# Idle-bank products of ones in eight pauses of TensorE, in a fused four-layer kernel

## The reference

```python
hidden = gelu(x @ down_W.T + down_b)                 # L0: adapter, 256 -> 64
hidden = hidden @ expert_W[idx].T + expert_b[idx] + domain_emb[idx]
x = layernorm(hidden @ up_W.T + up_b + x) * ln_gamma + ln_beta

x = _ln(src) * (1.0 + scale) + shift                 # L1: attention block, 16 heads of 16
scores = q @ k / sqrt(16) + attention_bias           # masked, softmax
x = x + (probs @ v) @ Wo + bo
ff = _gelu2((_ln(x) * g2 + beta2) @ W1 + b1) @ W2 + b2
x = x + ff                                           # L2: then a rotation of groups of four features

probs = softmax(style(norm(x)) @ router_w)           # L3: 8 experts, the best 2 of each token
y = sum over 2 experts of gate * (relu(h @ exp_w1 + exp_b1) @ exp_w2 + exp_b2)
return x + y
```

## Time and profile before

| | us |
|---|---|
| median of 3 runs | 686.25 |
| lowest, highest | 685.91, 686.96 |
| the profiled execution | 689.78 |
| its span | 687.9 |
| TensorE busy (share of the span) | 557.8 (81%) |
| VectorE busy | 468.5 (68%) |
| ScalarE busy | 297.2 (43%) |
| GpSimd busy | 226.5 (33%) |
| mean granted TensorE clock | 0.93 of full speed |

### The profile page before, as it was taken

How to read it: one execution, slowest core, us unless ns; L and a number is a source line. 1 busy time by engine, 2 the same in 40 slices (tenths; PEclk the granted TensorE clock), 3 DMA queues, 4 the chain that set the end, 5 groups by cost and what they waited for, 6 DMA issues and landing times.

```text
span 687.9 us, 15375 instructions
## 1 busy us (share of the span) xinstructions
PE 557.8 (81%) x4840; PEld 413.9 (60%) x4841; DVE 468.5 (68%) x1308; ACT 297.2 (43%) x616; POOL 226.5 (33%) x137
## 2 busy tenths in 40 slices
PE   3719576999597997769949399999789999999992
PEld 1616355558385484654838248676567778777771
DVE  5573796689979979883897935886454646474751
ACT  1615542642564425535243232666364444353540
POOL 0412553207714238133370422122612313122222
PEclk9999668999988999989978599999999999999996
DMA  8583451913066451466606576773532322222220
GB/s 288 127 203 124 156 158 56 226 32 123 1 170 160 131 184 63 130 149 227 200 1 244 210 253 232 274 260 49 171 48 41 50 40 42 33 48 38 43 42 0
DMA packets 41176, 86.49 MB, mean 126 GB/s; under 512 B 7321, under 2 KB 31810, under 8 KB 37026
## 3 DMA queue, kind: packets, MB, share of 16 engines
q1 hardware_dynamic: 21744, 56.77, 24.1%
q0 software_dynamic: 8352, 16.99, 13.4%
q10 hardware_dynamic: 11026, 12.02, 5.9%
HBM read 57.23 MB, written 29.44 MB: 126 GB/s over the span
## 4 chain that ended last, share of the span: by engine, by line
PE 53%; DVE 24%; issue 7%; ACT 5%; DMA 5%; ACTq 3%; POOL 2%; SPq 0%; DVEq 0%; POOLq 0%
PE bank L1918 8%; PE bank L1743 6%; PE bank L1907 5%; PE bank L1909 5%; PE bank L1908 4%; PE bank L1919 4%; PE bank L1642 3%; PE bank L1707 2%; PE bank L1723 2%; DMA stage<-in_moe_w 2%; PE bank L1752 2%; PE bank L1697 2%; ACTq L855 2%; DVE stats L1038 2%; DVE sc_sum L1127 2%
## 5 line engine op out<-in xcount | busy, mean ns | idle before, releaser
L1907 PE MATMUL bank<-xs_f,w_moe 128*128 128x128 f16 x624 | 123.3, 221 | 11.0 <-issue 6.6
L1909 PE MATMUL bank<-xs_f,w_moe 128*128 128x128 f16 x624 | 123.6, 221 | 2.7 <-issue 2.7
L867 ACT ACTIVATE stage<-bank,cols 128x128 f32<-128x128 f32 x312 | 88.3, 373 | 81.7 <-PE bank L1909 39.3
L1908 PE MATMUL bank<-xs_f,w_moe 128*128 128x128 f16 x624 | 122.8, 220 | 0.7 <-issue 0.7
L646 POOL DMA_INDIRECT out_x<-x_kept,ids x39 | 62.6, 1606 | 171.3 <-DVE x_kept L1511 122.3
L1907 PEld LDWEIGHTS bank<-xs_f,w_moe 128*128 x624 | 61.1, 98 | 47.0 <-issue 19.2
L1918 PE MATMUL bank<-w_moe,split 128*128 x208 | 79.3, 384 | 0.6
L1908 PEld LDWEIGHTS bank<-xs_f,w_moe 128*128 x624 | 61.4, 98 | 3.6 <-issue 0.8
L1909 PEld LDWEIGHTS bank<-xs_f,w_moe 128*128 x624 | 61.2, 98 | 3.5 <-issue 2.5
L1743 PE MATMUL bank<-w_moe 128*128 128x512 f32 x128 | 59.6, 627 | 3.2 <-ACT w_moe L745 3.2
L1005 DVE SCALAR_TENSOR_TENSOR split<-stage,split 128x2048 f16<-128x2048 f32 x16 | 41.4, 2585 | 30.4 <-ACT split L685 30.4
(11 more groups left out here) (273 smaller groups left out, 1186.8 us busy)
## 6 DMA issues: line engine op xcount, KB each, us to landing
stage<-in_moe_w SPq DMA_DIRECT2D x16, 1024.0 KB, 7.7
w_split<-split SPq DMA_DIRECT2D x16, 1024.0 KB, 4.9
w_moe<-w_split SPq DMA_DIRECT2D x8, 2048.0 KB
w_moe<-in_bias POOLq DMA_DIRECT2D x8, 1024.0 KB, 11.6
xs<-dispatched ACTq DMA_DIRECT2D x41, 130.0 KB
w_moe<-in_x_f SPq DMA_DIRECT2D x4, 512.0 KB, 7.1
w_moe<-in_x_t SPq DMA_DIRECT2D x4, 512.0 KB, 8.0
out_x<-x4b ACTq DMA_DIRECT2D x4, 512.0 KB
```

What stands on the lines that cost most here:

```text
L867: ins = act.activation(h32[j][:, f, :], bank[banks + g][:, P * (f % 4):P * (f % 4) + P], ACT.Relu, bias=moe_b1[:, bass.ds(e, 1), f], scale ...
L1907: pe.matmul(o, hi, xs_f[j][:, k, :], start=(k == 0), stop=False)
L1908: pe.matmul(o, hi, xs_f[j][:, KD + k, :], start=False, stop=False)
L1909: mm = pe.matmul(o, lo, xs_f[j][:, k, :], start=False, stop=(k == KD - 1))
```

## The change

A helper issues `count` matmuls of `ones` (stationary, 128x128 f16) by `ones` spread to 512 columns (moving), each into the same whole bank, without a wait and without a semaphore. It runs at eight places of TensorE's order: four outside the loop, and four in it (after `context(c + 1, 0)` for c = 0, 1 and 2, and for c = 2 also ahead of it).

```diff
+            def keep_clock(free_bank, count):
+
+                for _ in range(count):
+                    pe.matmul(bank[free_bank][:], ones[:], ones[:].unsqueeze(1).broadcast_to([P, 4, P]),
+                              start=True, stop=True)
+
...
             up_projection(0)
+            keep_clock(6, 38)
             turn1(0)
...
             scores(0, 1)
+            keep_clock(5, 14)
             pe.wait_ge(biased[1].sem, biased[1].of(0, 4))
             down_projection(1)
...
             turn1(1)
+            keep_clock(5, 10)
             queries(1)
             keys(1)
...
+                if c + 2 == NCH:
+                    keep_clock(4, 9)
                 context(c + 1, 0)
+                keep_clock(4, (15, 8, 14)[c])
                 turn3(c)
...
             c = NCH - 1
+            keep_clock(1, 14)
             turn2(c)
```

## The result

| | us |
|---|---|
| before, median of 22 runs | 686.46 |
| changed, median of 22 runs | 683.75 |
| ratio, 95% interval | 0.9961 (0.9945 to 0.9977) |
| changed, profiled execution, span | 685.26, 683.5 |

The change is 2.7 us faster, half of the 5.2 us that the sum booked; 683.75 lies inside the range of 676.8 to 685.3. One of the 22 runs of the changed kernel, 714.5 us at a granted clock of 0.824, was in a slower state, and the ratio goes by the others.

What follows compares the result with a forecast made beforehand. TensorE (53% of the chain) was taken to restart at half clock after pauses, with VectorE (24%) limiting gains. Terms 0.7 + 0.5 + 0.7 + 1.6 + 1.0 + 0.6 + 0.1 = 5.2 us took 686.25 to 681.0; range 676.8 to 685.3.

Steps and rivals of the forecast that it cites:

- Price of a filler, places, hiding engines: Eight TensorE places: 0.22 us per product at full clock, 0.43 at 1.2 GHz; gains only where VectorE or ScalarE wait.
- the 46.4 us that the prediction names as a sign of being wrong: At turn1(0), chunk 0: a start later than 46.4 us would show the prediction wrong.
- booked 1.6 of 1.8: turn2(3) and chunk 3's first feed-forward layer: full worth 1.8 us, times 0.9, 1.6 booked.
- nothing at down_projection(1): ScalarE's table load hides a sooner product; between 0 and 0.8 us possible, 0.1 booked.
- The full worth of each block: Gain if warm: queries(1) 1.6 us, turn3 blocks c = 0, 1, 2 1.2, 0.8, 1.6, before any discount.
- Does the remaining idle keep the clock?: Behind fillers, 2.3 to 2.7 us idle, just short of falls at 2.6 to 4.4; 0.6 to 0.65 per single pause.
- If it still falls, the next work is hurt no more: Behind the fillers: a clock that still falls does so later, hurting the next work no more than now.
- The second one: Rests lose the clock, only feed-forward 3 gains, or VectorE takes gains back: 0 to 1.3 us, 685.6; chance 0.13.
- Constant products do raise the clock: Denied by the slower rival: fillers stay at half clock, turn1(0) comes 3.3 us late, 689.6 us; chance 0.06.
- The overrun: Slower rival's mechanism: 38 products at 0.43 us take 16.3 us in the 13.03 us pause ahead of turn1(0).
- On transposes: Rival: transposes neither hold nor raise the clock, three turn3 blocks lose their 1.9 us, 682.9; chance 0.08.
- The 679.5: Time in us if cold turn3 stretches cost half their length: 2.8 at c = 2, 1.4 at c = 1.

Runs made afterwards that it cites:

- g3: The unchanged kernel from before, traced a second time: 686.48 us, one run.
- e3: Changed kernel with filler counts raised so 0.3 to 0.6 us stay idle, last 14 unaltered: 680.32 us, ratio to before 0.9922.
- e2: Changed kernel without the last 14 products ahead of turn2(3), all other fillers kept: 686.63 us, ratio to before 1.0002.
- e4: e3 plus 11 products between turn1(0) and queries(0): 678.77 us, ratio to before 0.9898.
- f1: As e3 but with fewer products, so 1.1 to 1.6 us stay idle behind the fillers: 684.01 us, ratio to before 0.9912.
- e1: Changed kernel with only the last fillers kept, 14 products ahead of turn2(3): 683.84 us, ratio to before 0.9979.
- f3: Kernel before plus only the first block's fillers, 48 ahead of turn1(0) and 11 ahead of queries(0): 688.77 us, ratio to before 0.9978.
- f4: e4 plus fillers in thin stretches (domain_experts(1), rank, behind turn2 of chunks 2 and 3), 16 at the end: 682.24 us, ratio to before 0.9895.
- g1: f1's counts without the filler ahead of down_projection(1), plus 9 products ahead of queries(0): 678.00 us, ratio to before 0.9870.

## Why the prediction was half right

- **Price of a filler, places, hiding engines: right.** 0.22 us at full clock and up to 0.43 at half; turn1(0) was not delayed by its fillers (2.35 us of rest left). It did start later than the 46.4 us that the prediction names as a sign of being wrong, at 47.57, but up_projection(0) ahead of the fillers was already 1.15 us late, and turn1(0) of the unchanged kernel starts at 47.33 in g3. Turn2(3) came 0.2 us later behind output_projection(3) than before (20.11 us against 19.88), hidden behind ScalarE's wait, and its block gained 2.1 us (booked 1.6 of 1.8); nothing at down_projection(1).
- **The full worth of each block: right**, as e3 shows: 1.5, 1.2, 0.9, 1.8 against 1.6, 1.2, 0.8, 1.6. VectorE had the room that its waits showed.
- **"Does the remaining idle keep the clock?": the step that failed.** I took 0.45 to 0.65 a block, from six falls that came 2.6 to 4.4 us after the last product, against rests of 2.3 to 2.7. In the changed kernel's trace none of these four blocks (booked 1.0 + 0.7 + 0.5 + 0.7 = 2.9) kept it throughout; together they gave 1.4, of which 1.0 at c = 2, and over three traces of each code nothing is left of it. With 2.2 to 3.0 us idle the clock was lost in 10 of 12 places, with less than 1.8 in none of 24. A fall "after the last product" was the wrong ruler: the clock can also fall when work has begun again (0.4 us into turn3(0)), so a rest shorter than the shortest fall is no safe one. The two short pauses read the earlier trace rows should have weighed more: one of 2.11 us had lost the clock.
- **"If it still falls, the next work is hurt no more": right for the block, not safe for what follows.** Feed-forward(2), whose evictions hold up the weight load, lost its clock in both traces of the changed kernel (15.54 and 15.55 us), which cost 1.5 us that stood in no term; it was warm in e2, the same code up to there, and in all three traces without the fillers. That the fillers moved the fall there is likely and not shown.
- **The rivals.** The second one (chance 0.13: the remaining idle lets the clock fall, and only the block without a remainder gains) had the mechanism. It was priced at 0 to 1.3 us, too little for the last block's own 1.6 to 1.8. Constant products do raise the clock: the 14 ahead of turn2(3) began at 1.2 GHz and ended at full clock (window 385.80 to 391.37, mean 0.54, turn2 at 1.04 us behind it). The overrun came in e4 and f1, from a clock lost before. On transposes, the clock of the kernel before rose at 281.48 with nothing but transposes since its fall. The Trainium skill (TensorE: Matmul & The Clock Gate, Part 4: PE-mode transpose) says that they don't count as busy for the clock in the same way as other products; this trace disagrees. The price that the Trainium skill (TensorE: Matmul & The Clock Gate, Terms and HAM oscillation) puts on a cold stretch, here half its length, gave 1.4 and 2.8 us for c = 1 and 2; e3's warm turn3 blocks are worth 0.9 and 1.8. The 679.5 that the prediction puts beside this price can't be had from its two figures: 0.65 x 0.6 and 0.45 x 1.2 less than 681.0 is 680.1.

What stays open: why `scores` loses the clock while TensorE is busy in some traces and not in others (it did in e1, whose first block is the unchanged kernel's, so the fillers are not needed for it), why feed-forward(2) is warm in some traces and cold in others, and what makes the same load take 7.0 or 8.5 us. None of these was tried.

## What to carry to other kernels

When a filler is to hold the clock, leave little of the pause: rests below 1.8 us kept it here in all 24 places that left them, and rests of 2.2 us or more returned nearly nothing, 108 products for no measurable gain, while five or six more in each place were worth some 3 us. Put fillers only where the block behind them is on the chain and where they still fit at half clock, because the clock may be lost before they start. And judge by medians of many runs: in a kernel with many thin stretches the clock falls at other places from trace to trace of the same code, and one such fall (1.5 us at feed-forward(2)) weighs as much as a filler gains.

## What the runs showed of the hardware

The clock fell while TensorE was busy: in e1 at 67.7 us, e4 at 66.3, f1 at 66.6, f3 at 63.8, f4 at 64.9 and g1 at 65.2, within products of 32 rows by 64 columns of weights with no gap above 0.4 us; in the other traces the same products kept it. Products of constant ones hold the clock (25 of them, then a rest of 0.36 us and turn3(0) at 1.09 in e3) and raise it (the 14 ahead of turn2(3)). And a load of 1 MB of expert weights at the same place took 7.04 to 7.06 us in six traces and 8.30 to 8.56 in five, and not by the clock of the layer ahead of it.
